# A gated cross-attention and feed-forward block: every second rounded sigmoid kept in DRAM between the two passes, and the up weight turned during the gate stage

## The chip, the cores and the metric

The kernel runs on one core of one Trainium2 chip. The metric is the device time of one execution in microseconds (us). The core's engines are TensorE (PE in the rows), VectorE (DVE), ScalarE (ACT), GpSimd (POOL) and SyncE, whose queue (SP) issues nearly all DMA transfers. Each works through its own list of instructions in order, and they meet by semaphores. Sixteen DMA engines move the data.

## The reference

Input x is (4, 1024, 512). A cross-attention (16 heads, not touched here) adds to it. Then the feed-forward part runs on N = 4096 rows of 512, with I = 1536 inner columns and every intermediate rounded to 16 bits with one scale for the whole tensor:

```
def act_qdq(x):
    scale = max(max(|x|) / 32767, 1e-12)
    return clip(round(x / scale), -32768, 32767) * scale
def fixed_qdq_u16(x):
    return clip(round(x * 65536), 0, 65535) / 65536
x = act_qdq(layernorm(x))
up   = act_qdq(x @ lpbq_dequant(w_up).T)
gate = act_qdq(x @ lpbq_dequant(w_gate).T)
sig  = fixed_qdq_u16(sigmoid(gate))
gate = act_qdq(gate * sig)
o    = act_qdq(gate * up)
out  = x + tanh(g_ffn) * (o @ lpbq_dequant(w_down).T)
```

lpbq_dequant rounds a weight to 4 bits in blocks of 32. Each act_qdq needs the largest magnitude of its whole tensor before its first element can be rounded, so `gate * sig` is gone over twice: once for its maximum, once to be made.

## The kernel before

Attention takes the first half of the time. Then the feed-forward part runs in four stages.

**Gate stage.** 48 tiles u = 12 cp + ot: column group cp (1024 of the 4096 rows of x) and output block ot (128 of 1536). A tile is 24 matmuls (`project`, L1046): two halves of 512 columns, each 12 terms of high and low 16-bit parts. ScalarE evicts a tile (`evict`, L1280), VectorE takes its largest magnitude and its highest value (L1704, L1708), SP stores it in `gate_scratch` (L815). Beside it the next column group of x is prepared: SP loads a tile of 128 rows (`load_x`), VectorE centres and rounds it, ScalarE and VectorE make its high and low half (`xs`), SP turns it with a DMA transpose into `x_hl` (`turn_x`, L748). `x_tile(u, lag)` says which tile is due; the turn of the last one of a group stands in tiles 10, 22 and 34, and the matmuls of the next group wait for it by halves. Also beside it the up and down weights are rounded, split in two 16-bit parts (`wh`) and stored (`wt_scratch`). Their steps stand in the table of `other_weight_jobs` (L88), by the tile u in which each engine does them; SP runs a tile's jobs, then stores the tile, then loads and turns x.

**Up stage.** 48 steps 4 ot + cp, again 24 matmuls each. The block's weight `Wu` (two buffers by two parts) is turned by two DMA transposes from `wt_scratch` every fourth step (`load_wu`, L821). Beside it runs the gate's work on 48 tiles of 128 x 1024, two in a step by `GATE_PLAN`. First pass, 24 steps: load the tile, round it to 16 bits (`gq`, L1343), sigmoid (L1316), round the sigmoid (`sgq`, L1751), largest of the product (L1777). Then the maximum is exchanged, and the second pass runs: sigmoid again, round again, product rounded in place (L1757), stored (`store_gated`), and turned to its magnitude (`signless`, L1331). Four of the 48 are left to the next stage by the tables `LATE_...`.

**Product stage.** When the largest of `up` is known, ScalarE rounds the magnitudes of `up` unit by unit, a unit being two tiles loaded back from `up_scratch` (`load_product`, `up_abs` L1369, six buffers), and VectorE takes the largest of each product with the gated tile (L1802).

**Down stage.** `o` is made in chunks and multiplied with the down weight, by TensorE's pace.

TensorE's psum has four banks of a tile, so tile k waits for the eviction of tile k-4; there are three eviction buffers, so eviction k waits for store k-3.

Of the kernel before, what the change touches and what calls it, by code (L numbers as in the profile page):

```python
# [30 lines left out]
NGT, NSG = 3, 2  # L31
NUW, NUD, NUQ, NXR = 6, 5, 3, 3
LATE = 4
# [55 lines left out]
def other_weight_jobs():  # L89
# [6 lines left out]
    for m, u in ((1, 0), (2, 22)):  # L96
# [6 lines left out]
        for k in range(OT):  # L103
# [4 lines left out]
            put(u + 11 + k, "wstore", m, k)  # L108
    return jobs
# [222 lines left out]
class Kernel:  # L332


    def __init__(self, nc, ctx, x, ctx_in, gx, gf, wg, wu, wd, cos_d, sin_d, id_d, bias_d, out):
# [10 lines left out]
        self.gated_d = nc.dram_tensor("gated_scratch", (OT, N // GW, 128, GW), I16).ap()  # L346
        self.up_d = nc.dram_tensor("up_scratch", (OT, N // GW, 128, GW), F32).ap()
        self.wt_d = [[nc.dram_tensor(f"wt{m}{j}_scratch", shape, F16).ap() for j in range(2)]
                     for m, shape in enumerate(((I, H), (I, H), (H, I)))]

# [98 lines left out]
        self.sgq = [A(f"sgq{i}", [128, GW], U16) for i in range(NSG)]  # L449
# [41 lines left out]
        self.d_xt = [sem(f"d_xt{i}") for i in range(NXS)]  # L491
# [107 lines left out]
def gate_plan():  # L599

    plan, done = [], 0
    for step in range(1, 49):
        until = 2 * min(step, 46)
        plan.append(range(done, until))
        done = until
    assert done == 96 - LATE
    return plan
# [18 lines left out]
LATE_SIGMOID = {-1: (44, 45), 13: (46,), 14: (47,)}  # L626
LATE_GATED = {7: (44,), 9: (45,), 15: (46,), 17: (47,)}
LATE_STORED = {12: (44,), 14: (45,), 19: (46,), 20: (47,)}
LATE_SIGNLESS = {-1: (40, 41), 11: (42, 43), 15: (44,), 17: (45,), 22: (46,), 23: (47,)}
# [36 lines left out]
def sync_program(e, K):  # L666
# [81 lines left out]
    def turn_x(n):  # L748
        e.wait_ge(K.v_xlo, n + 1)
        e.dma_start_transpose(K.x_hl[:, :, 128 * n:128 * n + 128], K.xs[n % NXS][:, :]).then_inc(K.d_xt[n % NXS], 16)  # L750
# [68 lines left out]

    def load_wu(ot):  # L820
        if ot == 0:  # L821
            e.wait_ge(K.pe_prj, 36)
            for h in range(2):
                for i in range(2):
                    e.wait_ge(K.d_wh[h][i], 16 * 12)
        if ot >= 2:
# [7 lines left out]
    for cp in range(4):  # L834
        for ot in range(OT):
            for job in TILE_JOBS.get(12 * cp + ot, []):
                if job[0] == "wload":
                    load_weight(*job[1:])
                if job[0] == "wstore":
                    store_weight(*job[1:])  # L840
            if (cp, ot) == (3, 6):
# [16 lines left out]
    def load_wd(part, j):  # L858
# [6 lines left out]
        e.dma_start_transpose(K.Wd[part][:, :, rows], K.wt_d[2][part][rows, :]).then_inc(K.d_Wd, 16)  # L865

# [30 lines left out]
    for ot in range(OT):  # L897
        if ot + 1 < OT:
            load_wu(ot + 1)
        for cp in range(4):  # L900
            store_projection((ot, cp), K.up_d)
            for n in GATE_PLAN[4 * ot + cp]:
                if n + 2 < 48:
                    load_gate(n + 2)
            for n in stored_in(4 * ot + cp):
                store_gated(n)
# [1192 lines left out]
```

## Time and profile before

| | |
|---|---|
| median of 3 runs | 1779.48 us (1778.51 to 1779.94) |
| the profiled execution's own time | 1775.83 us |
| its span | 1774.0 us, 24911 instructions |
| PE busy | 1633.1 us (92%) |
| DVE busy | 1467.2 us (83%) |
| ACT busy | 1249.5 us (70%) |
| gate stage | about 944 to 1187 us |
| up stage | 1187 to 1446 us |
| product stage | 1449 to 1516 us |
| down stage | 1522 us to the end |

The stages are read from the time line of TensorE and VectorE. Busy shares are averages over stages with different limits; what a change is worth is read from the stage it stands in.

### The profile page before, as it was taken

Reading aid. Unit: us, or ns where it says so; the run is one execution under the profiler, and the core shown is the slowest. Engines: PE = TensorE matmul, PEld = TensorE weight load, DVE = VectorE, ACT = ScalarE, POOL = GpSimd, SP = SyncE. Lnnn points to the kernel's source line nnn. Section 1 sums busy time; section 2 is a strip of 40 time slices with the busy share of each in tenths; the row PEclk is TensorE's granted clock in tenths of the full one; section 3 lists DMA queues with packets and bytes.
Section 4 is the critical chain, followed back from the end, with each engine's and each line's share of the span. In section 5 each row is a group of like instructions: output and inputs, shape, how many; then the busy total and the mean of one; then the engine's idle time right before and its main releaser. Section 6 shows DMA issues by size and latency. Waiting matters only on the chain. (4 is left out here: it accounts for less than half of the span.)

```text
span 1774.0 us, 24911 instructions
## 1 busy us (share of the span) xinstructions
PE 1633.1 (92%) x8677; PEld 603.5 (34%) x8677; DVE 1467.2 (83%) x2106; ACT 1249.5 (70%) x1965; POOL 835.7 (47%) x504
## 2 busy tenths in 40 slices
PE   3999999999999999999979999999999930899999
PEld 0232332232322332322225444444444410344444
DVE  7899999999999889888757998868989999764451
ACT  3688888888889888998753332329998998754440
POOL 5699899998999999998730110200000000000000
PEclk9999999999999999999989999999999975899999
DMA  6678878878688787778468898758985789986661
GB/s 154 154 145 176 158 169 178 170 164 179 140 179 179 147 172 162 164 148 158 90 160 225 247 256 253 220 163 283 301 278 201 243 299 390 301 274 217 225 215 59
DMA packets 370222, 354.57 MB, mean 200 GB/s; under 512 B 217104, under 2 KB 288144, under 8 KB 362160
## 3 DMA queue, kind: packets, MB, share of 16 engines
q1 hardware_dynamic: 361168, 287.97, 57.5%
q0 software_dynamic: 8928, 65.02, 18.8%
q8 instruction: 68, 1.11, 0.3%
q14 instruction: 58, 0.48, 0.1%
HBM read 147.78 MB, written 89.13 MB: 134 GB/s over the span
## 5 line engine op out<-in xcount | busy, mean ns | idle before, releaser
L1425 DVE TENSOR_REDUCE cm<-quad 128x1 f16<-128x1024 f32 x512 | 600.6, 1215 | 67.2 <-PE quad L967 67.1
L1204 ACT ACTIVATE P<-quad 128x512 f32<-128x512 f32 x1024 | 556.7, 598 | 124.0 <-PE quad L979 121.8
L2025 POOL TENSOR_TENSOR Ps<-P,P 128x2048 f32<-128x2048 f32 x93 | 430.6, 4630 | 53.1 <-ACT P L1204 53.0
L979 PE MATMUL quad<-QA,KA 101*128 101x512 f16 x1024 | 354.3, 387 | 6.1 <-ACT P L1204 5.0
L967 PE MATMUL quad<-KA,QA 100*128 100x512 f16 x1024 | 317.3, 391 | 25.4 <-DMA QA<-S 18.1
L1029 PE MATMUL quad<-P,cg 128*32 128x512 f32 x2048 | 272.9, 605 | 0.0
L1057 PE MATMUL quad<-x_hl,Wg 128*128 128x512 f16 (+1 forms) x1200 | 249.6, 371 | 5.6 <-DMA x_hl<-xs 4.6
L1057 PE MATMUL quad<-x_hl,Wu 128*128 128x512 f16 x1152 | 249.0, 380 | 0.3 <-DMA Wu<-wt_scratch 0.3
L1118 PE MATMUL quad<-Wd,oh 128*128 128x512 f16 x768 | 228.8, 380 | 0.0
L979 PEld LDWEIGHTS quad<-QA,KA 101*128 101x128 f16 x1024 | 83.6, 97 | 360.7 <-ACT P L1204 294.6
L1285 ACT ACTIVATE ev<-quad 128x1024 f32<-128x1024 f32 x95 | 96.2, 1013 | 125.7 <-PE quad L1057 119.7
L1057 PEld LDWEIGHTS quad<-x_hl,Wg 128*128 128x128 f16 x1200 | 116.9, 98 | 138.3 <-issue 7.7
L1057 PEld LDWEIGHTS quad<-x_hl,Wu 128*128 128x128 f16 x1152 | 112.5, 98 | 136.6 <-DMA Wu<-wt_scratch 0.8
L1706 DVE TENSOR_REDUCE mxt<-ev 128x1 f32<-128x1024 f32 x95 | 115.4, 1215 | 39.3 <-ACT ev L1285 39.0
L967 PEld LDWEIGHTS quad<-KA,QA 100*128 100x128 f16 x1024 | 99.1, 98 | 143.1 <-DVE cm L1425 41.8
L1118 PE MATMUL quad<-Wd,ol 128*128 128x512 f16 x384 | 145.7, 380 | 0.0
L1972 POOL TENSOR_TENSOR wq<-wl,wsc 128x512 f32<-128x512 f32 x36 | 40.8, 1134 | 216.8 <-DVE wl L1563 216.8
L1316 ACT ACTIVATE sgm<-gq,qs 128x1024 f32<-128x1024 int16 x96 | 109.7, 1146 | 9.4 <-DVE sgq L1751 7.8
L1848 DVE SCALAR_TENSOR_TENSOR xr<-quad,qs,xr 128x512 f32<-128x512 f32 x32 | 23.9, 750 | 110.1 <-PE quad L1118 105.4
L1394 ACT ACTIVATE oh<-oq 128x512 f16<-128x512 int16 x96 | 60.0, 625 | 66.4 <-DVE oq L1822 46.3
L1118 PEld LDWEIGHTS quad<-Wd,oh 128*128 128x128 f16 x768 | 75.1, 98 | 90.8 <-issue 0.3
L1002 PE MATMUL quad<-Ps,ones 128*32 128x512 f32 x776 | 101.9, 597 | 2.6 <-POOL Ps L2025 1.7
(167 smaller groups left out, 1899.1 us busy)
## 6 DMA issues: line engine op xcount, KB each, us to landing
Ps<-P POOLq DMA_DIRECT2D x62, 1024.0 KB, 7.7
gate_scratch<-ev SPq DMA_DIRECT2D x48, 512.0 KB, 3.5
gt<-gate_scratch SPq DMA_DIRECT2D x48, 512.0 KB, 5.2
up_scratch<-ev SPq DMA_DIRECT2D x48, 512.0 KB, 3.0
ud<-up_scratch SPq DMA_DIRECT2D x96, 256.0 KB, 3.6
x_words<-up_scratch SPq DMA_DIRECT2D x45, 512.0 KB, 11.3
gated_scratch<-gq SPq DMA_DIRECT2D x48, 256.0 KB, 2.8
gd<-gated_scratch SPq DMA_DIRECT2D x96, 128.0 KB, 4.1
```

Source lines behind the costliest of these rows:

```text
L967: mm = e.matmul(K.bank(use, c), K.QA[p % 2][0:100, 4 * qc + qt, h, :], K.KA[p % 2][0:100, 4 * c:4 * c + 4, h, :], start=True, stop=True)
L979: e.matmul(K.score[h % 2], K.KA[p % 2][0:101, kt, h, :], K.QA[p % 2][0:101, 4 * qc:4 * qc + 4, h, :], start=True, stop=True).then_inc(K.pe ...
L1002: mm = e.matmul(K.den[32 * h:32 * h + 32, :], K.ones[:, :], K.Ps[n % 2 if hf == NHALF - 1 else n][:, h, :], start=n == 0, stop=n == (3 if ...
L1029: mm = e.matmul(K.num[32 * h:32 * h + 32, :], K.cg[(p + 1) % 4][:, kt, 32 * h:32 * h + 32], K.Pb[before.g % NP][:, h, :], start=kt == 0, s ...
L1057: mm = e.matmul(K.quad[z][:, o:o + w], W(part, c), K.x_hl[:, x, c0:c0 + w], start=n == 0, stop=n == 11)
L1118: mm = e.matmul(ps, o[k][:, ot, sl], K.Wd[r][:, ot, :], start=ot == m == 0, stop=ot == OT - 1 and m == 2)
L1204: e.activation(K.Pb[pb][:, h, :], K.score[h % 2], ACT.Exp, scale=SCALE / (QPOW * KPOW)).then_inc(K.a_exp, 1)
L1285: e.activation(K.ev[k % NEV][:, :], K.quad[k % 4][:, :], ACT.Copy).then_inc(K.a_ev, 1)
L1316: e.activation(K.sgm[i % NSG][:, :], view(n), ACT.Sigmoid, scale=sg).then_inc(K.a_sig, 1)
L1425: e.tensor_reduce(cm[:, col:col + 1], K.quad[UNIT["max", hm, u] % 2][:, :], AX.X, ALU.max).then_inc(K.v_max, 1)
L1706: e.tensor_reduce(K.mxt[:, col:col + 1], K.ev[k % NEV][:, :], AX.X, ALU.max, apply_absolute_value=True).then_inc(K.v_mx, 1)
L2025: e.tensor_tensor(K.Ps[n][:, :, :], K.Pb[(st.g - 1) % NP][:, :, :], K.Pb[st.g % NP][:, :, :], ALU.add).then_inc(K.g_sum, 1)
```

## The change

It does three things. (a) In the first pass the rounded sigmoid of every second tile (the even ones) is stored to DRAM (`sig_scratch`), and in the second pass loaded back into one of four buffers; only the odd tiles have their sigmoid made again. (b) The plan of the gate's work is spread anew: the first pass over 25 steps, the second over 21, none left for the product stage; the magnitudes (`signless`) follow three steps behind and the last three stand in the product stage. (c) The up weight is turned in the gate stage, tiles 13 to 24, into the two `Wu` buffers that lie idle there, stored from them in turned form (`wu_scratch`) in tiles 15 to 26, and loaded from there by plain transfers in the up stage.

```
         put(u + 11 + k, "wstore", m, k)
+        if m == 1:
+            put(u + 13 + k, "wturn", k)
+            put(u + 15 + k, "wreturn", k)
...
-        until = 2 * min(step, 46)
+        until = 48 * step // 25 if step <= 25 else 48 + 48 * min(step - 25, 21) // 21
...
-    first, last = [max(0, min(2 * (u - 26), 40)) for u in (step - 1, step)]
+    first, last = [max(48, GATE_PLAN[max(u - 3, 0)].stop) - 48 for u in (step - 1, step)]
...
+    def turn_weight(k):
+        z = k % 2
+        if k >= 2:
+            e.wait_ge(K.d_Wu[z], 64 * (k // 2))
+        for i in range(2):
+            e.wait_ge(K.d_wh[z][i], 16 * (6 + k // 2 + 1))
+            e.dma_start_transpose(K.Wu[z][i][:, :, :], K.wt_d[1][i][128 * k:128 * k + 128, :]).then_inc(K.d_Wu[z], 16)
+    def return_weight(k):
+        z = k % 2
+        e.wait_ge(K.d_Wu[z], 64 * (k // 2) + 32)
+        for i in range(2):
+            e.dma_start(K.wu_d[k, i], K.Wu[z][i][:, :, :]).then_inc(K.d_Wu[z], 16)
     def load_wu(ot):
...
-            e.dma_start_transpose(K.Wu[ot % 2][i][:, :, :], K.wt_d[1][i][128 * ot:128 * ot + 128, :]).then_inc(K.d_Wu[ot % 2], 16)
+            e.dma_start(K.Wu[z][i][:, :, :], K.wu_d[ot, i]).then_inc(K.d_Wu[z], 16)
...
+    def store_sigmoid(j):
+        e.wait_ge(K.v_sgq, 2 * j + 1)
+        e.dma_start(K.sig_d[j, :, :], K.sgq[j % 2][:, :]).then_inc(K.d_short[j % 2], 16)
+    def load_sigmoid(q):
+        t = GATED[KEPT[q]]
+        if q == 0:
+            for z in range(2):
+                e.wait_ge(K.d_short[z], sig_stored_no(22 + z))
+        if q < NSL:
+            e.wait_ge(K.v_gmax, 48)
+        else:
+            e.wait_ge(K.v_g2, KEPT[q - NSL] + 1)
+        e.dma_start(K.sgl[q % NSL], K.sig_d[t // 2, :, :]).then_inc(K.d_short[q % NSL], 16)
...
+        elif i - 48 in MADE:
+            r = MADE.index(i - 48)
+            e.wait_ge(K.v_gmax, 48)
+            if r > 0:
+                e.wait_ge(K.v_sgq, 48 + r)
+            e.activation(K.sgm[0][:, :], view(GATED[i - 48]), ACT.Sigmoid, scale=sg).then_inc(K.a_sig, 1)
...
     def gated(n):
+        v = view(GATED[n])
+        if n in KEPT:
+            q = KEPT.index(n)
+            e.wait_ge(K.d_short[q % NSL], sig_loaded_no(q))
+            sig = K.sgl[q % NSL]
+        else:
+            if n > MADE[0]:
+                e.wait_ge(K.v_g2, MADE[MADE.index(n) - 1] + 1)
+            round_sigmoid(49 + MADE.index(n), 2, 0)
+            sig = K.sgq[2][:, :]
+        e.scalar_tensor_tensor(v, sig, sc["r2"], v, ALU.mult, ALU.mult).then_inc(K.v_g2, 1)
```

The first place is SP's queue in the gate stage, tiles 15 and 16 of 48. Each group of rows ends with the store of the gate tile; `xf` and `x_hl` are load and turn of x, `wh` the split weight, `wl` the weight's load. Before:

```order
L818 DMA gate_scratch<-ev_161 128x1024 [waits a_ev]
L745 DMA xf_151<-x_scratch 128x512 [waits v_xlo]
L750 DMA_TRANSPOSE x_hl<-xs_156 128x8x128 [waits v_xlo]
L738 DMA wt_scratch<-wh_132 128x512 [waits a_wh]
L738 DMA wt_scratch<-wh_133 128x512 [waits v_wl]
L723 DMA wl_126<-in_L_ffn_w_up_dram 128x512 [waits g_wq]
L818 DMA gate_scratch<-ev_162 128x1024 [waits a_ev]
```

Now, the same tiles:

```order
L836 DMA gate_scratch<-ev_161 128x1024 [waits a_ev]
L763 DMA xf_151<-x_scratch 128x512 [waits v_xlo]
L768 DMA_TRANSPOSE x_hl<-xs_156 128x8x128 [waits v_xlo]
L850 DMA wu_scratch<-Wu_166 128x512 [waits d_Wu1]
L850 DMA wu_scratch<-Wu_167 128x512
L844 DMA_TRANSPOSE Wu_166<-wt_scratch 128x4x128 [waits d_wh10,d_Wu1]
L844 DMA_TRANSPOSE Wu_167<-wt_scratch 128x4x128 [waits d_wh11]
L756 DMA wt_scratch<-wh_132 128x512 [waits a_wh]
L756 DMA wt_scratch<-wh_133 128x512 [waits v_wl]
L741 DMA wl_126<-in_L_ffn_w_up_dram 128x512 [waits g_wq]
L836 DMA gate_scratch<-ev_162 128x1024 [waits a_ev]
```

Four instructions have come in between the turn of x and the stores of the split weight. The transposes wait on the semaphore (`d_Wu1`) that the two stores ahead of them raise when they have landed; this group stands so in each tile from 15 to 24.

The second place is ScalarE in the second half of the up stage, its last steps and the begin of the product stage (`ev` eviction, `sgm` sigmoid, `gq<-gq` magnitude, `x_shorts` conversion of up). Before:

```order
L1285 ACTIVATE ev_161<-quad 128x1024
L1316 ACTIVATE sgm_171<-gq,qs 128x1024
L1316 ACTIVATE sgm_172<-gq,qs 128x1024
L1331 ACTIVATE gq<-gq 128x1024 x2
L1285 ACTIVATE ev_162<-quad 128x1024
```

Now:

```order
L1340 ACTIVATE ev_161<-quad 128x1024
L1375 ACTIVATE sgm_171<-gq,qs 128x1024
L1388 ACTIVATE gq<-gq 128x1024 x3
L1340 ACTIVATE ev_162<-quad 128x1024
L1388 ACTIVATE gq<-gq 128x1024 x2
L1382 ACTIVATE ev_163<-quad 128x512
L1384 ACTIVATE ev_163<-quad 128x512
L1388 ACTIVATE gq<-gq 128x1024 x2
```

One sigmoid has gone from most steps, and the two halves of the last eviction (L1382, L1384) now follow each other.

## Rows read from the trace of the kernel before

**Rows 1.** Time line of SP, gate stage: start, duration, queue, line, operation, tiles.

```profile
1026.95 0.43 SPq L818 DMA_DIRECT2D gate_scratch<-ev  x1
1027.42 0.43 SPq L745 DMA_DIRECT2D xf<-x_scratch  x1
1027.90 2.04 SPq L750 DMA_TRANSPOSE x_hl<-xs  x1
1029.98 1.44 SPq L738 DMA_DIRECT2D wt_scratch<-wh  x2
1031.47 0.45 SPq L723 DMA_DIRECT2D wl<-in_L_ffn_w_up_dram  x1
1031.96 0.45 SPq L818 DMA_DIRECT2D gate_scratch<-ev  x1
...
1059.60 2.13 SPq L750 DMA_TRANSPOSE x_hl<-xs  x1
```

**Rows 2.** Engine time by stretch, gate stage (busy us, granted clock, DMA share, GB/s).

```profile
1032.40:1043.40 11.00, 11.00 (x52) 4.98 (x51) 10.86 (x17) 4.34 (x6) 2.10 (x3) 1.00 1.04 312
```

**Rows 3.** Time line of TensorE, gate stage, from 1001 to 1130 us.

```profile
1064.84 62.32 PE L1057 MATMUL quad<-x_hl,Wg 128*128 128x512 f16 x288 [1.18 <-DMA x_hl<-xs]
```

**Rows 4.** DMA issues, 1015 to 1060 us: count, size, median us to landing.

```profile
wt_scratch<-wh SPq DMA_DIRECT2D x16, 128.0 KB, 2.5
```

**Rows 5.** Up stage: Wu's transposes on SP, and two stretches without and with them.

```profile
1303.50 2.51 SPq L829 DMA_TRANSPOSE Wu<-wt_scratch  x2
```

```profile
1298.10:1303.50 5.40, 5.40 (x27) 2.45 (x26) 5.04 (x8) 5.34 (x6) 0.00 (x0) 1.00 0.86 299
1303.50:1308.80 5.30, 5.30 (x26) 2.36 (x25) 4.94 (x8) 4.88 (x6) 0.00 (x0) 1.00 1.21 258
```

**Rows 6.** TensorE alone by stretch (clock before the share), and its warm-up later.

```profile
1438.00:1440.00 2.00, 0.00 (x0) 0.95 0.74 277
1440.00:1442.00 2.00, 0.00 (x0) 0.50 0.86 278
```

```profile
1516.99 5.10 PE L1068 MATMUL quad<-Wd 128*128 128x512 f16 x12
```

**Rows 7.** The matmuls of the up stage: durations, first and last start.

```profile
L1057 PE MATMUL quad<-x_hl,Wu x1152: 378/380/390, 1187.1 to 1436.0; 128*128 128x512 f16 x192
```

**Rows 8.** Time line of ScalarE, first half of the up stage.

```profile
1295.10 1.00 ACT L1285 ACTIVATE ev<-quad 128x1024 f32<-128x1024 f32 x1
...
1300.45 1.00 ACT L1285 ACTIVATE ev<-quad 128x1024 f32<-128x1024 f32 x1
```

**Rows 9.** Time line of VectorE, second half of the up stage.

```profile
1373.51 1.21 DVE L1706 TENSOR_REDUCE mxt<-ev 128x1 f32<-128x1024 f32 x1
1374.64 0.69 DVE L1751 TENSOR_SCALAR sgq<-sgm 128x1024 uint16<-128x1024 f32 x1
1375.36 1.28 DVE L1757 SCALAR_TENSOR_TENSOR gq<-sgq,qs,gq 128x1024 int16<-128x1024 uint16 x1
1376.57 0.69 DVE L1751 TENSOR_SCALAR sgq<-sgm 128x1024 uint16<-128x1024 f32 x1
```

**Rows 10.** Time line of ScalarE, end of the up stage.

```profile
1445.28 0.58 ACT L1327 ACTIVATE ev<-quad 128x512 f32<-128x512 f32 x1
...
1448.93 3.23 ACT L1369 ACTIVATE x_shorts<-ev,qs 128x1024 int16<-128x1024 f32 x3 [1.17 <-DVE qs L1669]
```

**Rows 11.** Time line of VectorE, product stage, and the row behind its last reduction.

```profile
1451.26 1.26 DVE L1802 CUSTOM_DVE_ANT_0 quad<-x_shorts,gq 128x1024 f32<-128x1024 int16 x1
...
1452.44 1.26 DVE L1802 CUSTOM_DVE_ANT_0 quad<-x_shorts,gq 128x1024 f32<-128x1024 int16 x1
...
1516.08 0.20 DVE L1655 TENSOR_REDUCE red<-mxt 128x1 f32<-128x48 f32 x1
```

**Rows 12.** ScalarE's conversions in the product stage, and DMA from 1450 to 1510 us.

```profile
1458.55 2.00 ACT L1369 ACTIVATE x_shorts<-x_words,qs 128x2048 int16<-128x2048 f32 x1 [0.72 <-DMA x_words<-up_scratch]
1461.26 2.00 ACT L1369 ACTIVATE x_shorts<-x_words,qs 128x2048 int16<-128x2048 f32 x1 [0.71 <-DMA x_words<-up_scratch]
```

```profile
DMA packets 12053, 23.42 MB, mean 390 GB/s; under 512 B 754, under 2 KB 754, under 8 KB 12051
```

More of the change, by code:

```diff
@@ L448, in __init__ @@
         self.sgm = [A(f"sgm{i}", [128, GW], F32) for i in range(NSG)]
-        self.sgq = [A(f"sgq{i}", [128, GW], U16) for i in range(NSG)]
+        self.sgq = [A(f"sgq{i}", [128, GW], U16) for i in range(NSQ)]
+        late = nc.alloc_sbuf_tensor_at("sg_late", [128, 2, GW], U16, offset=A.at - 2 * NSQ * GW - 4 * GW)
+        self.sgl = [self.sgq[0][:, :], self.sgq[1][:, :], late[:, 0, :], late[:, 1, :]]
         self.ident16 = A("ident16", [128, 128], F16)
@@ L490, in __init__ @@
         self.d_rows = [sem(f"d_rows{i}") for i in range(NXF)]
-        self.d_xt = [sem(f"d_xt{i}") for i in range(NXS)]
+        self.d_short = [sem(f"d_short{i}") for i in range(NXS)]
         self.d_ev = [sem(f"d_ev{i}") for i in range(NEV)]
@@ L904, in sync_program @@
                     load_gate(n + 2)
+            for n in GATE_PLAN[4 * ot + cp - 1] if ot + cp > 0 else ():
+                if n < 48 and n % 2 == 0:
+                    store_sigmoid(n // 2)
+            if 4 * ot + cp == 25:
+                for q in range(NSL):
+                    load_sigmoid(q)
             for n in stored_in(4 * ot + cp):
                 store_gated(n)
+                if n in KEPT and KEPT.index(n) + NSL < 24:
+                    load_sigmoid(KEPT.index(n) + NSL)
             if ot == OT - 1:
@@ L1323, in evict_last @@
         e.activation(K.ev[k % NEV][:, 0:512], K.quad[k % 4][:, 0:512], ACT.Copy).then_inc(K.a_ev, 1)
-        for n in LATE_SIGMOID[-1]:
-            sigmoid(GATED[n], 48 + n)
         e.wait_ge(K.pe_prj, 97)
@@ L1344, in scalar_program @@
                     e.wait_ge(K.a_gq, n + 1)
-                    sigmoid(n, n)
+                    sigmoid(n)
                     if n == 1:
@@ L1352, in scalar_program @@
                 else:
-                    sigmoid(GATED[n - 48], n)
+                    sigmoid(n)
             for n in signless_in(4 * ot + cp):
@@ L1375, in scalar_program @@
         up_abs(i)
-        for n in LATE_SIGMOID.get(i, ()):
-            sigmoid(GATED[n], 48 + n)
-        for n in LATE_SIGNLESS.get(i, ()):
-            signless(n)
+        if i > 5 and i % 2 == 0 and SIGNLESS + i // 2 - 3 < 48:
+            signless(SIGNLESS + i // 2 - 3)
     def quantize_up(n):
@@ L1734, in vector_program @@
                     round_weight(*job[1:])
-                else:
+                elif job[0] not in ("wturn", "wreturn"):
                     weight_now(job)
@@ L1804, in vector_program @@
             m += 1
-        for n in LATE_GATED.get(i, ()):
-            gated(n)
     e.wait_ge(K.v_pmax, 48)
```

78 lines of the change are left out of this document (39 added, 39 removed).

## The prediction

> **What bounds the kernel now.** I read the table of engine time by stretch first, then the time line of each engine in the stages that the change touches, then the sync engine's own queue, because the change moves mostly transfers and their issues. There are three stages to keep apart.
>
> In the gate stage (48 tiles of 24 matmuls, from about 944 us) TensorE runs without a gap inside a column group of twelve tiles: twelve tiles take 62.32 us, and it waits 1.18 us at the third group's border for the turned tiles of x, a transfer [rows 3]. That turn is issued by SP at 1059.60 [rows 1]. So the sync queue (SP) has no slack there: whatever delays it at that point delays TensorE one for one. The same rows of SP show a tile period, 1026.95 to 1031.96, filled without a gap. And the 16 DMA engines are at 1.04 of their time in that stretch [rows 2].
>
> In the up stage TensorE runs from 1187.1 to 1436.0 [rows 7] at 5.19 us a step; the first of its two halves has ScalarE at 5.35 us a step (from eviction to eviction) [rows 8], the second VectorE at 4.97 us (1.13 for the largest, twice 0.72 for rounding and 1.21 for the gated product) [rows 9]. Both had fallen behind: TensorE's last matmul starts at 1436.0, but the last half tile is evicted only at 1445.28, and the product stage starts at 1448.93 [rows 7, 10]. That stage is VectorE's: 48 reductions at a pitch of 1.18 us, four late gated products between them, end at 1516.08 [rows 11]. ScalarE converts one unit of two tiles each 2.71 us there, waiting for its load each time [rows 12]. The down stage follows TensorE alone and is not touched.
>
> **The change part by part. 1: the second pass of the sigmoid.** 24 of 48 second sigmoids go from ScalarE and 24 roundings from VectorE. A second-pass step now has 48/21 = 2.29 tiles, half of them stored: VectorE 1.13 + 2.29 x (1.21 + 0.36) = 4.73 us [rows 9], against 5.19 of TensorE. After the exchange of the maximum between the halves VectorE is some 9 us behind (an estimate, from 4 us of small instructions and the lag ahead of them); 0.46 us a step over 20 steps wins 9.2 back, and the last two steps hold no gated product. So the last eviction can follow TensorE: 1436.0 + 0.4 + 0.58 = 1437.0 instead of 1445.28 + 0.58 = 1445.9 [rows 7, 10]. Gain 8.9; bounds 4 (if half of the lag stays) and 8.9, since nothing can be evicted before it is computed.
>
> **2: no late gated products.** Four pairs of 0.72 + 1.21 leave the product stage: 7.7 us [rows 9]. Is something next? The loads come at 2.71 us a unit [rows 12] and VectorE then needs 2 x 1.18 = 2.37 [rows 11], so they become the later pace if they start where they did. But the first units are fetched in the last four steps, by a queue that no longer lags: about 10 us earlier, while 22 units lose 22 x 0.34 = 7.5 to VectorE. They stay just ahead. The 0.25 MB stores of the four late tiles also leave this stream. I take 8.1, with part of the small idle; if the loads start no earlier it is 8 less 7.5, about 0.5. Parts 1 and 2 give 17 us, between 5 and 18. The Trainium skill ("DMA: Bandwidth & Descriptors", Specifications) puts HBM for one core at about 358 GB/s; the product stage shows 390 [rows 12], so the measurement decides; by the page a unit would take 2.93 us and my sum would lose about 2 us.
>
> **3: 24 stores and 24 loads of sigmoids.** They add 0.25 MB to a first-half step that moves about 1.5 MB with a DMA share of 0.86, so about 0.14 of share; the steps with Wu's transposes show 1.21 and lose them [rows 5]. I take zero; at worst 0.3 us in each of 25 steps, 7 us. In the second half DMA is far emptier. The first four loads wait for the last store, but VectorE has the maximum's exchange and one tile with its own sigmoid before it needs one.
>
> **4: Wu turned in the gate stage.** This is the large term. At u = 13 to 24 SP issues two DMA transposes, at u = 15 to 26 two stores back to DRAM, and, as the order of the queue shows, in one tile the stores of weight k-2 stand directly ahead of the transposes of weight k into the same buffer, which wait for these stores to land. Behind that wait stand, on the same in-order queue, the stores of the split weight, the load of the next weight, the store of the gate tile, the load of x and the turn of x. A period of SP in tiles 16 to 22 is then, by pitches of rows 1: gate store 0.47, x load 0.48, x turn 2.08, two returns 0.94, wait for landing 2.5 - 0.5 = 2.0 (the nearest row is the equally large store of the split weight, 2.5 us from issue to landing [rows 4]), two transposes 2.51 (the same instruction in the up stage [rows 5]), two weight stores 0.94, weight load 0.48: 9.9 us. Tiles 19 to 21 have no weight load and 21, 22 no x load: 67.4 us for the seven. Before, they run at VectorE's pace, 38.2 us. The difference is 29.2. The tile ahead, with a return and a wait but no x turn, adds 3; and the turns of x should issue faster when the rings have drained during the wait, for which I take 2 off (an estimate). So the turn of the group's last x tile leaves about 30 us late, at 1090 instead of 1059.60, and TensorE, which has no slack there, stops for 30 us in tile 24.
>
> From below: by SP alone nothing makes a tile shorter than about 8.2 (x turns at 1.3, all waits at 1.9), 21 us; from above, landing behind a queued x turn costs 1 us more a tile, 37 us. The buffers ahead (three of evictions, four banks) don't help, since the border needs x itself. After tile 24 the queue has at most two more such tiles and catches up by tile 27, so the next border (at tile 36) moves by 0 to 1.
>
> **5: TensorE's clock.** After its idle the granted clock is 0.50, that is 1.2 GHz, 4 us after the last matmul; on restart twelve warm-up matmuls took 5.10 us, where twelve at the full pitch of 0.216 take 2.6 [rows 6]. A stop of 30 us brings that once: 2.5 us, between 0 and 5.
>
> **6: Wu in the up stage** now comes by plain loads of 128 KB, one step ahead; TensorE did not wait for it and won't: zero.
>
> **Sum.** 30 + 2.5 - 17 = +15.5 us. The profiled execution took 1775.8 us by its own time (span 1774.0), which makes 1791.3; the median of the timed runs stands 3.7 above it, so on that scale 1779.5 + 15.5 = 1795.
>
> **The rivals.** *The queue hides the round trip (faster).* If the stores back landed while SP was still issuing, or SP's part-empty periods took the new issues, no border would move and only the gains would be left: 1779.5 - 17 = 1762.5. For it: most of SP's time line is short issues. Against it: the waiting instruction comes directly behind the stores it waits for, and 0.94 + 2.51 us of new issue alone do not fit into a 5.5 us tile whose SP share is already 4.45 (0.47 + 0.48 + 2.08 + 0.94 + 0.48). It decides if SP's tile stays under 5.5 + 17/8, about 7.5 us, for then stall and gain cancel. Chance 0.12.
>
> *The DMA engines set the pace, not the queue.* A pair of Wu transposes costs 1.21 x 5.3 - 0.86 x 5.4 = 1.8 us of all 16 engines [rows 5], a pair of returns (0.26 MB at 390 GB/s) 0.7. Added to 1.04 x 5.4 = 5.6 [rows 2] that is 8.1 us a tile. If waits overlap better than I think, this floor remains: seven tiles x (8.1 - 5.45) + 3 = 21.6 us, 1779.5 + 21.6 + 2.5 - 17 = 1786.6. Chance 0.12. The Trainium skill ("DMA: Bandwidth & Descriptors", in its table of errata) gives DMA transposes 261 GB/s with a non-contiguous middle dimension: a pair would cost 1.0 us instead of the 1.8 that the rows make, the floor would be 7.3 and the time about 1781. I follow the rows.
>
> *The stall comes and the gains do not.* The product stage becomes one of loads (2.71 us a unit), and ScalarE waits for the gate tiles that share the engines with sigmoids: gain 5 to 8, time 1779.5 + 32.5 - 7 = 1805. Chance 0.12.
>
> **How the numbers follow.** Forecast 0.64, its own range 1785 to 1804. The range of 8 in 10 leaves out most of the first rival: 1780 to 1807. Less than 0.2% (3.6 us) can't be told from no change. Faster: the first rival and a tail, 0.14; the same: 0.06, between it and the DMA floor; slower: 0.80.
>
> **What would show it.** On SP's time line a gap before each Wu transpose, ended by a return's landing, and 9 to 10 us between gate stores in tiles 16 to 22; one idle of TensorE of about 30 us behind tile 24's first half, released by the turn of x, with a granted clock of 0.50 behind it; from there every stage the same amount later until the up stage. There, the last eviction within 1.5 us of the last matmul, and about 57 us from the first to the last product reduction with no gated product in between. I am wrong in step 4 if gate stores stay under 7.5 us apart; in step 1 if the last eviction still trails by 4 us or more; in step 2 if VectorE waits for conversions more than 3 us in all in the product stage.

## The result and the profile after

The changed kernel takes 1824.76 us (median of 4 runs, 1822.74 to 1826.32) against 1779.71 for the kernel before (4 runs); the ratio is 1.0260, 95% interval 1.0248 to 1.0273. It is 45 us slower, where 15.5 were forecast. The profiled execution took 1822.74 us (span 1820.8), 46.8 us of span more than the profiled one of before.

The whole difference can be read along TensorE. Rows are start, duration, instruction, count and the idle time ahead with its releaser; first the time line after, from the border at tile 24 to the product stage:

```profile
1067.47 5.25 PE L1112 MATMUL quad<-x_hl,Wg 128*128 128x512 f16 x12 [4.90 <-DMA x_hl<-xs]
1104.90 64.87 PE L1112 MATMUL quad<-x_hl,Wg 128*128 128x512 f16 x288 [32.19 <-DMA x_hl<-xs]
1173.38 59.73 PE L1112 MATMUL quad<-x_hl,Wg 128*128 128x512 f16 x276 [3.60 <-DMA x_hl<-xs]
1232.94 124.64 PE L1112 MATMUL quad<-x_hl,Wu 128*128 128x512 f16 x576
1360.39 20.89 PE L1112 MATMUL quad<-x_hl,Wu 128*128 128x512 f16 x96 [2.81 <-DMA Wu<-wu_scratch]
1385.37 105.46 PE L1112 MATMUL quad<-x_hl,Wu 128*128 128x512 f16 x480 [4.09 <-DMA Wu<-wu_scratch]
1494.75 0.30 PE L1118 MATMUL quad<-ident,column 128*128 128x128 f32 x1 [3.92 <-DVE column L1551]
```

The same places before, beside [rows 3]:

```profile
1127.51 59.73 PE L1057 MATMUL quad<-x_hl,Wg 128*128 128x512 f16 x276 [0.35 <-DMA x_hl<-xs]
1187.08 165.92 PE L1057 MATMUL quad<-x_hl,Wu 128*128 128x512 f16 x768
1353.29 83.05 PE L1057 MATMUL quad<-x_hl,Wu 128*128 128x512 f16 x384 [0.29 <-DMA Wu<-wt_scratch]
1447.29 0.45 PE L1063 MATMUL quad<-ident,column 128*128 128x128 f32 x1 [10.94 <-DVE column L1498]
1516.75 0.45 PE L1063 MATMUL quad<-ident,column 128*128 128x128 f32 x1 [69.02 <-DVE column L1498]
```

| piece | forecast | measured |
|---|---|---|
| ahead of the change's place | 0 | +1.5 |
| waits at tile 24: 4.90 + 32.19 - 1.18 | +30 | +35.9 |
| wait at the next border: 3.60 - 0.35 | 0 to 1 | +3.3 |
| half clock in the gate stage: 5.25 for 12 matmuls instead of 2.6, 64.87 instead of 62.32 | +2.5 | +5.2 |
| up stage, 257.9 us instead of 249.3 | 0 | +8.6 |
| from TensorE's end to the first column transpose, 3.92 instead of 10.94 | -8.9 | -7.0 |
| product stage, 69.0 instead of 69.5 (1494.75 to 1563.74) | -8.1 | -0.5 |
| down stage | 0 | -0.2 |
| sum | +15.5 | +46.8 |

The down stage is counted from the column transpose that ends the product stage to the end of the span. So the stop was there, at the forecast place, and larger; of 17 us of gain 7.5 came; and the up stage, counted at nothing, took more than that back.

The sync queue in the gate stage after, the rows that answer to [rows 1]:

```profile
1017.94 0.45 SPq L836 DMA_DIRECT2D gate_scratch<-ev  x1
1018.91 1.57 SPq L850 DMA_DIRECT2D wu_scratch<-Wu  x2
1023.43 3.02 SPq L844 DMA_TRANSPOSE Wu<-wt_scratch  x2
...
1028.08 0.45 SPq L836 DMA_DIRECT2D gate_scratch<-ev  x1
...
1038.48 0.46 SPq L836 DMA_DIRECT2D gate_scratch<-ev  x1
1038.98 0.43 SPq L763 DMA_DIRECT2D xf<-x_scratch  x1
1039.45 2.02 SPq L768 DMA_TRANSPOSE x_hl<-xs  x1
1041.52 1.20 SPq L850 DMA_DIRECT2D wu_scratch<-Wu  x2
1044.81 2.50 SPq L844 DMA_TRANSPOSE Wu<-wt_scratch  x2
1047.36 1.05 SPq L756 DMA_DIRECT2D wt_scratch<-wh  x2
...
1048.96 0.43 SPq L836 DMA_DIRECT2D gate_scratch<-ev  x1
...
1099.28 1.80 SPq L768 DMA_TRANSPOSE x_hl<-xs  x1
```

Every issue of the forecast stands there with about its duration (the pair of returns 1.2 us instead of 0.94), and the gap of 2.1 us between 1042.72 and 1044.81 is the wait for the landing. The next one (1053.12 to 1057.41) is 4.3, of which the view of waits counts 3.9. That view, from 1000 to 1100 us, sums them (engine, line, releaser: total, times, longest):

```profile
SPq L844 <- DMA wu_scratch<-Wu: 17.1, 8, 3.9
```

Meanwhile the DMA engines were no longer full, so the queue and not they set the pace (stretch, busy us of PE, PEld, DVE, ACT, POOL, clock, DMA share, GB/s; compare 1.04 in [rows 2]):

```profile
1036.00:1046.40 10.40, 10.40 (x50) 4.70 (x48) 5.47 (x9) 2.17 (x3) 1.05 (x1) 1.00 0.71 199
1105.00:1110.00 5.00, 5.00 (x13) 1.70 (x13) 0.00 (x0) 0.00 (x0) 0.00 (x0) 0.50 0.41 90
```

The second row is TensorE behind the stop: 13 matmuls in 5 us, a granted clock of 0.50, that is 1.2 GHz, as in [rows 6].

### The profile page after: what moved, and what is told of

It reads as the page before. It is cut to its first block and busy times, and to the rows that moved or that the text cites. A ratio compares the mean times of both kernels' runs of the same rounds, so it can differ in the third digit from the quotient of the medians.

```text
span 1820.8 us, 25034 instructions
## 1 busy us (share of the span) xinstructions
PE 1641.2 (90%) x8677; PEld 605.2 (33%) x8677; DVE 1452.8 (80%) x2082; ACT 1224.6 (67%) x1941; POOL 836.4 (46%) x504
## 5 line engine op out<-in xcount | busy, mean ns | idle before, releaser
L1478 DVE TENSOR_REDUCE cm<-quad 128x1 f16<-128x1024 f32 x512 | 600.5, 1215 | 68.1 <-PE quad L1022 67.8
L1112 PE MATMUL quad<-x_hl,Wg 128*128 128x512 f16 (+1 forms) x1200 | 255.2, 376 | 43.4 <-DMA x_hl<-xs 42.7
L1440 ACT ACTIVATE uq<-ud,qs 128x512 int16<-128x512 f32 x96 | 68.1, 711 | 34.5 <-DMA gd<-gated_scratch 31.8
```

The source lines that it names most:

```text
L1112: mm = e.matmul(K.quad[z][:, o:o + w], W(part, c), K.x_hl[:, x, c0:c0 + w], start=n == 0, stop=n == 11)
L1440: e.activation(K.uq[n % NUQ][:, :], K.ud[n % NUD][:, :], ACT.Copy, scale=ru).then_inc(K.a_uq, 1)
L1478: e.tensor_reduce(cm[:, col:col + 1], K.quad[UNIT["max", hm, u] % 2][:, :], AX.X, ALU.max).then_inc(K.v_max, 1)
```

## The experiments

The kernels ran in four groups, each on one chip beside runs of the kernel before, so ratios to it are compared rather than times. Where two profiled executions are compared, differences of 2 to 4 us can stand in the gate stage even where both kernels have the same code there; the text says so where it matters.

**1. Without the early turning.** `Wu` is turned in the up stage again, all else is that of the changed kernel.

```
-                put(u + 13 + k, "wturn", k)
-                put(u + 15 + k, "wreturn", k)
...
-            e.dma_start(K.Wu[z][i][:, :, :], K.wu_d[ot, i]).then_inc(K.d_Wu[z], 16)
+            e.dma_start_transpose(K.Wu[ot % 2][i][:, :, :], K.wt_d[1][i][128 * ot:128 * ot + 128, :]).then_inc(K.d_Wu[ot % 2], 16)
```

> The changed kernel with the up weight turned in the up stage again, as before the change; the stored sigmoids and the new plan stay. Theory (the gate stage loses to the early turning alone): TensorE enters the up stage at about 1187 to 1189 us as before. The up stage then shows whether its 8.6 us come from the sigmoids' traffic: if they do, they stay or grow, since the transposes cost the DMA engines more than plain loads, TensorE waits 7 to 15 us for Wu, and the total is 1782 to 1790. Rival (Wu's plain loads are what comes late): TensorE waits for Wu as little as before (0.3 us), and the total is 1772 to 1775. If part of the gate stage's loss were the stored sigmoids', the total would be over 1795.

Measured: 1776.82 us, ratio 0.9987 (0.9977 to 0.9997). The gate stage is that of before (up stage entered at 1188.62), and TensorE waits for `Wu` 3.00, 2.56 and 0.33 us, at the end of the first half, as in the changed kernel. The theory's mechanism stands, its price was too high (5.9 us of waits where 7 to 15 were expected, 1776.8 us where 1782 to 1790 were): the kept sigmoids and the new plan make the kernel 0.1% faster, hardly more than nothing. And the loss in the up stage belongs to them, not to part 6 (plain loads in place of transposes), since it is there with the old transposes too.

**2. Only the early turning,** on the kernel before (the edit of 1 turned around).

> The kernel before with the early turning and the plain Wu loads alone; no stored sigmoids, old plan. Theory: all of the gate stage's loss comes back, TensorE enters the up stage 44 to 47 us late; in the up stage no wait for Wu (no sigmoid traffic), the last eviction trails by 10 us as before; total 1824 to 1828. Rival (the two parts add to each other's loss): under 1815.

Measured: 1827.94 us, ratio 1.0279 (1.0263 to 1.0294), as expected but for a small wait for `Wu`. The stop is 31.81 us behind one of 4.50, ScalarE waits for gate tiles 4.3 us, TensorE 1.51 for `Wu`, and the last eviction trails as before (12.17 us to the column transpose). Parts (a) with (b) and part (c) add up: 1.0279 x 0.9987 = 1.0265, against 1.0260 of the changed kernel.

**3. The return one tile earlier,** so that a whole tile lies between the two stores and the transposes that wait for them.

```
-                put(u + 15 + k, "wreturn", k)
+                put(u + 14 + k, "wreturn", k)
```

> The changed kernel with each turned weight stored back one tile after its transposes instead of two, so that the store that a transpose waits for was issued a tile earlier; the same instructions and bytes. Theory (the in-order queue waits for the return's landing, 2.2 us a tile, beside its own issues): the queue's period falls from 10.4 to about 8.2 us, the stop of TensorE by 15 to 22 us, total 1803 to 1810. Rival 1 (the DMA engines' time sets the pace): same period, 1825. Rival 2 (the wait was the whole loss): 1785 or less.

Measured: 1802.73 us, ratio 1.0137 (1.0122 to 1.0152): 22 us back from one number. TensorE:

```profile
1088.15 64.06 PE L1112 MATMUL quad<-x_hl,Wg 128*128 128x512 f16 x288 [24.51 <-DMA x_hl<-xs]
1152.81 59.73 PE L1112 MATMUL quad<-x_hl,Wg 128*128 128x512 f16 x276 [0.60 <-DMA x_hl<-xs]
```

No wait for a landing is left among the sync queue's waits, the gate stores stand 8.4 us apart (1025.69, 1034.05, 1042.53), and the next border's wait is gone too. The sum of issues alone (0.45 + 0.43 + 2.0 + 1.2 + 2.5 + 1.05 + 0.45 = 8.1) and the small gaps between them fill that period. TensorE's waits at tile 24 fell from 37.1 to 24.5 us, so about 12.6 of them came from landings; with the shorter wait at the next border and the second stretch at half clock gone, TensorE enters the up stage 20.6 us earlier (1212.38 instead of 1232.94). Of the 24.5 left, 1.2 are from before. The rest is issue by these rows; but the DMA engines are 0.84 busy over these seven tiles, where they were 0.70 with the waits, so they come close to a limit as well.

**4. The returns issued by GpSimd,** one tile earlier, the sync queue keeping the transposes only (`d_acc` are two semaphores that are free after attention).

```
-                if job[0] == "wreturn":
-                    return_weight(job[1])
...
+    # GpSimd, tile by tile
+            if job[0] == "wreturn":
+                return_weight(job[1])
```

> The changed kernel with the returns of the turned weight (to DRAM) issued by GpSimd's queue and one tile earlier; the sync queue issues the transposes alone. Theory (the stop at tile 24 is issue and waiting time of the sync queue, one for one): against the kernel with the return one tile earlier the sync queue loses 0.94 us a tile, from 8.4 to 7.5, so TensorE's stop falls from 24.5 to about 18, and the time is near 1802.7 - 6.5, 1795 to 1798. Rival A (the DMA engines' work sets it): the stop stays at 23 to 25 and the time at 1802. Rival B (GpSimd's stores are late, since its own weight jobs stand ahead, and the sync queue waits for their landing again): the stop is 25 to 32, the time 1803 to 1812.

Measured: 1803.33 us, ratio 1.0145 (1.0127 to 1.0163): no gain on experiment 3. TensorE goes on behind the stop at 1088.01 us, where it did at 1088.15; the stop reads 22.33 us instead of 24.51 only because TensorE came to it 2.0 us later. Two things took back what the queue had gained. In tile 15 it waited once for the landing of a return, now issued by GpSimd (view of the queue's waits from 1000 to 1100 us):

```profile
SPq L847 <- DMA wu_scratch<-Wu: 4.2, 1, 4.2
```

So this tile's gate store went out at 1028.60, 2.9 us later than in experiment 3. Behind it the seven tiles 16 to 22 took 53.3 us instead of 57.1, a gain of 3.9 where the theory had 0.94 a tile, 6.6. There the same pair of transposes takes 3.2 us to issue instead of 2.5,

```profile
1028.60 0.44 SPq L839 DMA_DIRECT2D gate_scratch<-ev  x1
...
1029.56 2.11 SPq L771 DMA_TRANSPOSE x_hl<-xs  x1
1031.77 3.19 SPq L847 DMA_TRANSPOSE Wu<-wt_scratch  x2
...
1036.59 0.45 SPq L839 DMA_DIRECT2D gate_scratch<-ev  x1
```

and over the first two periods, 1028.60 to 1044.57, the DMA engines are nearly full (0.86 busy in the same two tiles of experiment 3):

```profile
1028.60:1044.57 15.97, 15.97 (x75) 7.25 (x74) 10.99 (x18) 4.46 (x6) 4.19 (x6) 1.00 0.95 261
```

The period is 8.0 us, where the rival on the DMA engines put its floor at 8.1 from the shares of [rows 2, 5]. In the same two tiles the period was 10.4 us by the queue with landings, 8.4 with issues alone, and is 8.0 with the engines 0.95 busy: they look like the next limit, just below the queue. That full engines are what makes the transposes' issue longer is argued and not shown, since in [rows 5] a pair took 2.51 us at a share of 1.21. Rival A of the expectation holds by the time, rival B by one wait. The Trainium skill ("DMA: Bandwidth & Descriptors", Issuing engines are not separate DMA queues) says that another issuing engine doesn't bring other DMA engines, and saves only the time to issue; the trace agrees: over these two tiles the engines moved 261 GB/s, against 254 in experiment 3, and of the 1.2 us of the queue's time that a pair of returns had taken in each tile, 0.4 came back.

**5. Turning late:** transposes in tiles 33 to 44, the first three still ahead of the last border, returns a tile later.

```
-                put(u + 13 + k, "wturn", k)
-                put(u + 15 + k, "wreturn", k)
+                put(u + 33 + k, "wturn", k)
+                put(u + 34 + k, "wreturn", k)
...
-            if (cp, ot) == (3, 6):
+            if (cp, ot) == (3, 9):
```

> The changed kernel with the turning moved to tiles 33 to 44, the returns to 34 to 45, and the first Wu load to tile 45, where the queue and the DMA engines have room and hardly any x is turned. Same instructions and bytes. Theory (it is the place, beside the turns of x in a full queue, that costs): the gate stage loses 0 to 4 us, the up and product stages as in the changed kernel (+1 us in all), total 1780 to 1785. Rival (the work costs wherever it stands): 1800 or more.

Measured: 1784.14 us, ratio 1.0031 (1.0018 to 1.0044), as the theory had it. The stop at tile 24 is gone (1.64 us); at tile 36, behind the first transposes, TensorE waits 3.85 us for x instead of 0.35. Here returns follow by one tile, as in experiment 3, so against that one (1.0137) the later place, with the first load of `Wu` three tiles later, is worth 1%.

**6. The loads of the turned weight issued by GpSimd,** on the kernel of 5.

```
+    # GpSimd, behind its weight jobs
+    for ot in range(OT):
+        load_wu(ot)
```

> The kernel with the late turning (weight turned in tiles 33 to 44), and with the loads of the turned up weight issued by GpSimd's queue, which has nothing else to do in the up stage, instead of the sync queue. Theory (the up stage loses time because the sync queue is several tiles behind and issues the weight's load too late, not because the load is slow): TensorE's waits for Wu fall from 4.9 us in the kernel with the late turning to under 1, the up stage shortens by 4 to 5 us, and the time is 1784.1 - 4.5, about 1779 to 1781. Rival (the load itself is slow on engines that are 0.95 busy): the waits stay at 3 us or more and the time at 1783 to 1785.

Measured: 1787.07 us, ratio 1.0044 (1.0032 to 1.0056), no gain at all. The waits for `Wu` did fall to none. In their place, at the same tiles:

```profile
1319.11 5.34 PE L1102 MATMUL quad<-x_hl,Wu 128*128 128x512 f16 x24 [0.97 <-ACT ev L1330]
...
1332.29 10.71 PE L1102 MATMUL quad<-x_hl,Wu 128*128 128x512 f16 x48 [1.89 <-ACT ev L1330]
...
1372.87 77.87 PE L1102 MATMUL quad<-x_hl,Wu 128*128 128x512 f16 x360 [2.54 <-ACT ev L1330]
```

Seven such waits sum to 7.3 us. TensorE had run out of psum banks, so ScalarE was four tiles behind. My theory fell: the late weight was only the first face of that lag, and the sync queue, which waits for ScalarE's evictions (100.1 us in all from 1190 to 1450 us in the kernel of 5), was late because of it. The rival (slow transfers) fell as well.

**7. Sigmoids in narrow transfers,** on the kernel of 5.

```
+        w = GW if j in (0, 1, 2, 23) else 64
-        e.dma_start(K.sig_d[j, :, :], K.sgq[j % 2][:, :])
+        e.dma_start(K.sig_d[j, :, 0:w], K.sgq[j % 2][:, 0:w])
```

and the same with the loads. The kernel leaves out 960 of the 1024 columns of 20 of the 24 sigmoids; it only serves to tell the bytes of these transfers from their number.

> The kernel with the late turning, with 20 of the 24 sigmoid stores and of the 24 loads cut to 64 of 1024 columns (the rest of these sigmoids is left out, so the second pass multiplies by old values); waits, order and numbers of transfers are as before. Theory (the bytes of the sigmoids keep the DMA engines from feeding ScalarE its gate tiles, and so put the sync queue behind): ScalarE's waits for gt fall from 13.9 us to 2 to 5, TensorE's waits for Wu from 4.9 to under 1, the time is about 1777 to 1780, more if the product stage gets its loads earlier. Rival (the number of transfers or the new spread of the plan does it, not the bytes): gt waits stay above 10 us and the time at 1783 to 1785.

Measured: 1774.5 us, ratio 0.9979 (0.9967 to 0.9990), half a per cent under 5. TensorE:

```profile
1194.90 250.50 PE L1114 MATMUL quad<-x_hl,Wu 128*128 128x512 f16 x1152 [2.11 <-DMA Wu<-wu_scratch]
```

The up stage has no gap at all. ScalarE's rounding of the gate tiles, grouped by line (count, busy us, mean ns, idle ahead and its releaser): before, after, and this kernel.

```profile
L1343 ACT ACTIVATE gq<-gt,qs 128x1024 int16<-128x1024 f32 x48 | 54.6, 1137 | 2.4 <-DMA gt<-gate_scratch 2.2
```

```profile
L1400 ACT ACTIVATE gq<-gt,qs 128x1024 int16<-128x1024 f32 x48 | 54.6, 1139 | 14.3 <-DMA gt<-gate_scratch 14.1
```

```profile
L1402 ACT ACTIVATE gq<-gt,qs 128x1024 int16<-128x1024 f32 x48 | 54.6, 1138 | 7.1 <-DMA gt<-gate_scratch 6.8
```

And the landing of a gate tile in the first half of the up stage (count, size, median us), in the same order:

```profile
gt<-gate_scratch SPq DMA_DIRECT2D x42, 512.0 KB, 5.2
```

```profile
gt<-gate_scratch SPq DMA_DIRECT2D x38, 512.0 KB, 5.7
```

```profile
gt<-gate_scratch SPq DMA_DIRECT2D x40, 512.0 KB, 5.4
```

In the kernel of 5, with whole sigmoids, it is 5.9 us, and in experiment 2, with none, 5.2. So the sigmoids' bytes are the cause of the loss: half a microsecond more per landing, for an engine that needs a tile each 2.6 us and has no slack. What is left (6.8 us of waits instead of 2.2) is two or three tiles of lag, which fit in the four banks; the view of TensorE has no wait left. Whether the remainder is from the number of transfers or from the eight that stayed whole was not tried.

**8. The product stage's loads issued by GpSimd,** and the transposes of the down weight's first part four steps earlier, on the kernel of 5.

```
+    # GpSimd
+    for j in range(NU - 3):
+        load_product(j)
...
-            if cp == 1 and ot >= 8:
-                load_wd(0, ot - 8)
+            if cp == 1 and 7 <= ot < 11:
+                load_wd(0, ot - 7)
```

> The kernel with the late turning, with the loads of the product stage issued by GpSimd's queue, so that they don't stand behind the gated stores and the weight's transposes on the sync queue, and the four transposes of the down weight's first part one group of steps earlier. Theory (the product stage is a stream of loads that starts where the sync queue comes to it): the first loads go out 5 to 8 us before the last matmul of up, the product stage is 65 to 66 us instead of 68.2, and the time 1781 to 1782. Rival A (the 16 DMA engines are full in the last steps of the up stage too, so that an earlier issue only takes from other transfers): the stage shortens by under 1 us or TensorE loses as much before it; the time stays at 1783 to 1785. Rival B (GpSimd's queue issues and moves slower): the pitch of a unit rises above 2.8 us, the time above 1786.

Measured: 1788.18 us, ratio 1.0047 (1.0032 to 1.0062). The product stage did shrink, to 65.6 us from 68.2, but it began 9.60 us behind TensorE's end instead of 5.11: the loads now came ahead of the stores of gated tiles, for which ScalarE's magnitudes wait.

```profile
L1372 ACT ACTIVATE gq<-gq 128x1024 int16<-128x1024 int16 x45 | 45.0, 1045 | 9.8 <-DMA gated_scratch<-gq 9.8
```

This is rival A in kind, an earlier load only takes from another transfer, though the stage did shrink by more than its 1 us. The time (1788.2) is above that rival's 1783 to 1785, and not all of it is the edit's: the profiled execution is 4.8 us longer than that of 5, of which 2.9 stand ahead of the up stage, where both have the same instructions. The edit's own price is then about 2 us, and the two edits in it were not tried apart.

**9. All three together,** the weight turned in tiles 35 to 46 (weights 0 and 1 last, left in their buffers), both kinds of loads by GpSimd.

> All of it: sigmoids kept, the weight turned in tiles 35 to 46, behind the last border of the gate stage, with weights 0 and 1 turned last and left in their buffers (no store, no load), loads of the other ten and of the product stage by GpSimd. Theory: the gate stage is that of the kernel before (borders 1 to 2 us, entry into the up stage at about 1188 to 1190), TensorE waits under 1 us for Wu, the end of the up stage is at 1438 to 1440, the product stage 66 to 68 us; the time is 1766 to 1771. Rival (the DMA engines set the up stage's pace): 1773 to 1777, like the kernel without the early turning.

Measured: 1788.38 us, ratio 1.0046 (1.0031 to 1.0062): a miss. The border at tile 36 cost 0.33 us, but the entry into the up stage waited 3.23 for the last transposes, ScalarE's lag took 7.0 in waits for evictions, and the early product loads brought the 9.96 us of experiment 8 again. Three edits, each aimed at a wait that the trace names, gain nothing over the kernel of 5.

**10. The first pass over 26 steps,** on the kernel of 1.

```
-        until = 48 * step // 25 if step <= 25 else 48 + 48 * min(step - 25, 21) // 21
+        until = 48 * step // 26 if step <= 26 else 48 + 48 * min(step - 26, 21) // 21
```

> The kernel without the early turning, with the first pass over 26 steps instead of 25 (the second over 21 as before, so that it ends one step later). Theory (in the first half of the up stage ScalarE, at TensorE's own pace of 5.2 us a step, has nothing to make up its 14 us of waits for gate tiles with, and is passed on to TensorE when four psum banks are used up): each of 26 steps holds 0.07 tiles fewer, 0.16 us, so ScalarE's lag is some 4 us smaller; TensorE's waits fall from 5.9 to 1 to 3 us, the time from 1776.8 to 1772 to 1775. Rival (the waits come from the transposes of Wu themselves, late on full engines): waits stay at 5 to 6 us; the second pass, one step later, then costs 1 to 3 us at the end: 1777 to 1780.

Measured: 1777.75 us, ratio 0.9998 (0.9987 to 1.0009). TensorE's waits are 4.7 us instead of 5.9, and the column transpose comes 6.05 us behind its end instead of 4.63. What is given first is taken last: no gain, between theory and rival.

**11. As 10, with the down weight's transposes one group earlier** (the second edit of 8).

> The kernel before it (first pass over 26 steps), with the four transposes of the down weight one group of four steps earlier, so that the last group holds none. Theory (the transposes stand directly ahead of the first product loads on the sync queue, 4.7 us of issue): the product stream starts 2 to 4 us earlier and the product stage is 66 to 68 instead of 69.5, the time 1 to 3 us below that kernel. Rival (as with the product loads issued by GpSimd, the engines are full until the end of the up stage, and what starts earlier takes from gated stores): the last magnitudes wait for stores, and the time is the same within 1 us.

Measured: 1774.17 us, ratio 0.9980 (0.9967 to 0.9993). Compared with 10 the interval just excludes no change. On the sync queue of 10 this transpose stood between the first product loads and the rest:

```profile
1442.13 3.55 SPq L932 DMA_DIRECT2D x_words<-up_scratch  x4
1445.73 4.75 SPq L898 DMA_TRANSPOSE Wd<-wt_scratch  x1
```

In 11 it is gone from there, and the product stage takes 67.3 us instead of 68.9. But the column transpose ahead of it comes 7.70 us behind TensorE's end instead of 6.05, and the profiled execution of 11 enters the up stage 4.2 us earlier, though the edit doesn't touch the gate stage. The shorter stage is the move's; that the whole 0.2% is, these profiles don't show.

**12 and 13. The same move of these transposes,** in the kernel of 1 and in the kernel before, because it was open whether it pays only with kept sigmoids.

> The kernel without the early turning (first pass over 25 steps), with the four transposes of the down weight one group of four steps earlier. Theory (the product stream stands behind 4.7 us of a transpose's issue in the last group; the move was worth 3.6 us in the kernel with 26 steps): product stage 66.5 to 68 instead of 69.5, time 1773 to 1775, ratio 0.996 to 0.998 of before, which beats both kernels. Rival (what was measured there was the chip's run to run difference): 1776 to 1778.

> The kernel before, with only the four transposes of the down weight one group of four steps earlier. Theory (there the product stage is VectorE's, 1.18 us a product and four late gated products, so an earlier load stream brings nothing): the time is that of before within 1.5 us, ratio 0.999 to 1.001. Rival (the down weight's transposes disturb the last group in either kernel): the time falls by 2 to 4 us, ratio 0.998, and the kept sigmoids are worth nothing beyond it.

Measured: 1774.9 us, ratio 0.9982 (0.9970 to 0.9995) with the sigmoids kept, as the theory had it (without the move 0.9987, in another group, so what the move adds there is within the intervals), and 1776.05 us, ratio 0.9983 (0.9974 to 0.9993) in the kernel before. The move is worth 0.17% there by itself, so my theory for 13 fell and its rival stands: with it, keeping the sigmoids brings nothing that can be measured. The product stage is 68.1 us in 12, against 69.5 in 1, and that of before is 68.3 us with the move instead of 69.5, and VectorE waits 1.5 us for conversions in it instead of 2.4:

```profile
L1802 DVE CUSTOM_DVE_ANT_0 quad<-x_shorts,gq 128x1024 f32<-128x1024 int16 x48 | 57.0, 1258 | 1.5 <-ACT x_shorts L1369 1.5
```

Experiments 11, 12 and 13 beat the kernel before by two tenths of a per cent, and the changed one by 2.7; 13 does it with a change of two lines.

## Why the prediction was too small

**Direction and place were right, the size was not: 1795 forecast, range up to 1807, 1824.8 measured.** Step by step:

*Part 4, the sync queue: mechanism right, 30 us against 39.2 (35.9 at tile 24 and 3.3 at the next border).* The rows show the forecast order, the wait and its releaser. The seven periods of tiles 16 to 22 were put at 67.4 us (9.6 a tile; this holds only with a second weight load in tile 22, which the prediction doesn't name) and measured 70.7, 3.3 more: the waits for landings were 15.2 us in all where 14 were taken, one of them 4.3, and the seven pairs of returns took 8.3 us to issue where 6.6 were taken. The larger miss stands ahead of it. For the tiles before I allowed 3 us and took 2 off, for turns of x that issue faster behind the waits. Instead tiles 13 to 15 lost 5.6 us: their gate store moved from 1020.96 to 1028.08, of which 1.5 are from earlier. 0.9 of it fell in tiles 13 and 14, which have transposes and no return and which I did not count, and 4.7 in tile 15, with the first returns and a wait of 2.95. The 2 us taken off are in no run: tile by tile the turns of x took as long as before (2.1 us in tile 16, 1.5 in tiles 21 and 22, in both kernels). Together 38.1 instead of 30.2 (1.5 us of earlier lateness make 39.7, the move of the last turn, 1059.60 to 1099.28). I also held the next border safe to within 1 us; it lost 3.3, since x is loaded by the same late queue:

```profile
1122.39 0.55 DVE L1503 TENSOR_SCALAR xf<-xf,mv,rs 128x512 f32<-128x512 f32 x1 [3.57 <-DMA xf<-x_scratch]
```

The bounds of this term (21 to 37) hold the 35.9 of tile 24, but not the 39.2 of both borders: they varied the landings and not the tiles ahead or behind.

*Part 5, the clock: 5.2 us against 2.5.* The stop came in two, a wait of 4.90 us, twelve matmuls and one of 32.19. Each was followed by matmuls at 1.2 GHz, so the price was paid twice; the bound of 5 was right.

*Parts 3 and 6, counted at zero: 8.6 us, the step that failed in kind.* I compared the sigmoids' bytes with the free share of the DMA engines and took what is free for what is harmless. The mean share in the first half is 0.92 in both kernels, and yet gate tiles landed 0.5 us later (5.7 against 5.2). The equal mean hides two changes: with the plain loads of `Wu` and no sigmoids (experiment 2) it is 0.83, and with sigmoids and the old transposes (experiment 1) 1.00; the gate tiles landed in 5.2 and 5.8 us there. So the landing went with the sigmoids and not with the share. ScalarE stood at 5.35 us a step before [rows 8], and by the new plan of 25 steps at about 5.2 (an estimate: 0.08 tiles fewer in a step, at 2.2 us each), in steps of 5.19. It had nowhere to put 12 us more of waits. "At worst 7 us" was nearly the right bound and should have been the value. 6.6 us more of waits and 1.65 of clock (105.46 for 480 matmuls, 103.8 at full clock) reached TensorE. Experiments 1, 6 and 7 show that it is the bytes by way of ScalarE, not the source of `Wu`.

*Part 1: 7.0 against 8.9, held.* The last eviction's halves start at 1491.76 and 1492.23, 0.9 and 1.4 us behind TensorE's end at 1490.83, against 8.9 in [rows 7, 10]. The rest of the term went into two magnitudes that now stand between it and the conversions:

```profile
1492.23 0.59 ACT L1384 ACTIVATE ev<-quad 128x512 f32<-128x512 f32 x1
1492.71 2.00 ACT L1388 ACTIVATE gq<-gq 128x1024 int16<-128x1024 int16 x2
1496.24 3.23 ACT L1426 ACTIVATE x_shorts<-ev,qs 128x1024 int16<-128x1024 f32 x3 [1.53 <-DVE qs L1722]
```

*Part 2: 0.5 against 8.1.* The forecast named both ends, "8 less 7.5, about 0.5, if the loads start no earlier", and chose the other. They started no earlier: the first four loads went out 7.9 us ahead of the first column transpose (8.5 before), the next two 2.4 behind it (0.5 before). The queue had kept its place, and the last gated stores and a transpose of 4.7 us stood ahead of the stream.

```profile
1486.83 2.67 SPq L933 DMA_DIRECT2D x_words<-up_scratch  x4
1489.56 4.71 SPq L899 DMA_TRANSPOSE Wd<-wt_scratch  x1
1494.31 0.58 SPq L836 DMA_DIRECT2D up_scratch<-ev  x1
1494.99 2.06 SPq L921 DMA_DIRECT2D gated_scratch<-gq  x3
1497.14 1.51 SPq L933 DMA_DIRECT2D x_words<-up_scratch  x2
```

The stage is one of loads now, with 65.5 us from the first to the last reduction where about 57 were forecast; VectorE waits for conversions 7.3 us in all (2.4 before), the bound that the prediction had set for being wrong here was 3:

```profile
L1864 DVE CUSTOM_DVE_ANT_0 quad<-x_shorts,gq 128x1024 f32<-128x1024 int16 x48 | 57.9, 1250 | 7.7 <-ACT x_shorts L1426 7.3
```

Experiment 8 shows that it could not be had by issuing earlier from GpSimd either: ScalarE then waited 9.8 us for the gated stores. The rival "the stall comes and the gains do not" was the true one in kind; it named ScalarE's waits too, but with all of them it still kept 5 to 8 us of gain, where 7.5 of gain less 8.6 in the up stage leave a loss of 1, and so it stopped at 1805.

*Added up:* stop and clock were 12 us short (44.4 against 32.5), parts 3 and 6 8.6, parts 1 and 2 9.5, and 1.5 came from ahead of the change, together 31 us, less 0.2 in the down stage. The range held only the bound of one of these terms at a time; all of them at their worst (a stop of 37, a clock of 5, sigmoids 7, a gain of only 5) make 1823.5 us, close to what came. They share a cause, transfers added to a queue and to engines that were full, and so it was no chance, I think, that they moved together.

## What to carry to other kernels

In an in-order queue a transfer that waits for the landing of one just issued costs the landing for everything behind it; one tile of distance gave half of the loss back. A share of DMA time below one says nothing of a consumer without slack: ask by how much each landing grows and who has no reserve for it. When the trace names a late transfer, look whether its issuer was itself waiting for an engine that is behind, for then an issue from elsewhere only renames the wait.

## What the runs showed of the hardware

- The issue time of a pair of DMA transposes of 128 rows by 512 (16 bits) is no constant. It was 2.50 to 2.51 us in the changed kernel from tile 16 on, but 3.0 to 3.1 in its tiles 13 to 15, and from 2.5 to 3.9 in experiment 4, where GpSimd issued stores beside it. The share of the DMA engines alone does not explain it: 3.02 us were taken at a share of 0.44 (tile 15), 2.51 at 1.21 [rows 5].
- Stores of 128 KB landed in 2.0 us (the split weight) and 2.9 us (the turned weight) by the median in one and the same stretch (1015 to 1080 us), the latter up to 4.8.
- At the same mean share of the DMA engines, 0.92, a load of 512 KB landed in 5.2 us (before) or 5.7 us (after) by the median.
